# Values one step behind the next step's scores, and the second batch's keys one step later, in a four-layer kernel of window attention and experts

## The reference

```python
x = x + einsum('bct,bcd->bdt', x, weights[cond])        # layer 0: one 64x64 matrix per batch, over tokens
x = x + attention(x)                                     # layer 1: 8 heads, 4 kv groups, paged cache, window of 256
x = x + (einsum('bsi,bio->bso', x, W[id]) + b[id])       # layer 2: one of 16 experts (512x512) per batch
x = x + (x @ W3.T + scale * (x @ A[ad].T) @ B[ad].T)     # layer 3: dense 512x512 and an adapter of rank 16
```

```python
scores = einsum('bghtd,bgsd->bghts', qg, k_all) * SCALE
allowed = (kpos <= pos) & (kpos > pos - 256)
p = softmax(where(allowed, scores, -inf))
o = einsum('bghts,bgsd->bghtd', p, v_all);  out = o @ Wo.T
```

## Time and profile before

| | |
|---|---|
| median of 3 runs | 1145.85 us (1144.73 to 1155.21) |
| the profiled execution | 1151.32 us, of which the profile's span is 1149.5 us |
| PE busy over the span | 1043.8 us, 91% |
| PE weight loads | 702.4 us, 61% |
| DVE, ACT, POOL busy | 57%, 47%, 47% |
| granted clock of TensorE, mean | 0.962 |
| DMA, mean | 171 GB/s |

### The profile page before, as it was taken

How to read it: one execution, slowest core, us unless ns; L and a number is a source line. 1 busy time by engine, 2 the same in 40 slices (tenths; PEclk the granted TensorE clock), 3 DMA queues, 4 the chain that set the end, 5 groups by cost and what they waited for, 6 DMA issues and landing times.

```text
span 1149.5 us, 23649 instructions
## 1 busy us (share of the span) xinstructions
PE 1043.8 (91%) x6354; PEld 702.4 (61%) x6354; DVE 653.0 (57%) x1887; ACT 539.1 (47%) x1336; POOL 535.4 (47%) x601
## 2 busy tenths in 40 slices
PE   4999999997488999999899999998999999999997
PEld 2776777775355666656566566665655666656655
DVE  5889796667234555545455555555454554545552
ACT  3457766674333445434344444444354443434440
POOL 2555445368545545544544445544454545444400
PEclk9999999999559999989999999999899998999998
DMA  3343534553356666555656666666566666566640
GB/s 127 106 150 115 165 114 149 158 196 123 93 170 214 208 185 218 182 177 167 189 184 208 196 185 208 182 188 204 172 198 187 189 204 185 169 188 206 201 147 19
DMA packets 95335, 196.13 MB, mean 171 GB/s; under 512 B 31346, under 2 KB 40114, under 8 KB 87110
## 3 DMA queue, kind: packets, MB, share of 16 engines
q1 hardware_dynamic: 63942, 149.49, 40.0%
q0 software_dynamic: 30784, 44.16, 13.9%
q10 hardware_dynamic: 576, 2.10, 0.5%
HBM read 195.08 MB, written 33.56 MB: 199 GB/s over the span
## 4 chain that ended last, share of the span: by engine, by line
PE 62%; ACT 4%; issue 3%; another core or an unknown queue 3%; DMA 1%; POOL 1%; DVE 0%; ACTq 0%; POOLq 0%; DVEq 0%
PE bank L93 22%; PE bank L1341 10%; PE bank L1316 9%; PE bank L1303 8%; PE bank L1295 8%; PE bank L1282 4%; ACT KT L1101 2%; PE bank L1272 2%; ACT PT L1101 1%; DMA KV<-kv_scratch,idxs 1%; DMA KV<-in_pool,idxs 1%; ACT PR L1110 0%; POOL KV L1007 0%; POOL KVE L1017 0%
## 5 line engine op out<-in xcount | busy, mean ns | idle before, releaser
L1101 ACT ACTIVATE PT<-bank 112x384 f32<-112x384 f32 x256 | 113.5, 487 | 267.1 <-PE bank L1303 205.1
L1179 DVE CUSTOM_DVE_ANT_0 SM<-bank,FM 128x336 f32<-128x336 f32 x256 | 129.7, 507 | 168.1 <-PE bank L1295 131.1
L1017 POOL DMA_INDIRECT KVE<-kv_scratch,idxs_e x96 | 95.7, 997 | 124.9 <-DMA KVE<-in_pool,idxs_e 100.1
L1017 POOL DMA_INDIRECT KV<-kv_scratch,idxs x96 | 95.8, 998 | 119.4 <-DMA KV<-in_pool,idxs 99.9
L1110 ACT ACTIVATE PR<-SM,nb 128x336 f32<-128x336 f32 x256 | 145.4, 574 | 1.1 <-DVE nb L1183 0.9
L1007 POOL DMA_INDIRECT KV<-in_pool,idxs x96 | 95.0, 990 | 76.2 <-PE bank L1316 49.6
L1007 POOL DMA_INDIRECT KVE<-in_pool,idxs_e x90 | 88.9, 988 | 87.5 <-PE bank L1316 59.7
L1101 ACT ACTIVATE KT<-bank 128x336 f32<-128x336 f32 x128 | 57.5, 449 | 145.3 <-PE bank L1282 137.7
L1341 PE MATMUL bank<-W,XT 128*64 128x512 f32 x512 | 123.7, 604 | 0.7 <-ACT XT L1101 0.7
L1295 PE MATMUL bank<-KT,QB 64*128 64x336 f32 x512 | 112.9, 519 | 11.2 <-ACT KT L1101 9.0
L1303 PEld LDWEIGHTS bank<-ident,PR 128*112 128x112 f32 x768 | 85.1, 137 | 48.7 <-issue 47.8
(11 more groups left out here) (173 smaller groups left out, 2139.7 us busy)
## 6 DMA issues: line engine op xcount, KB each, us to landing
W<-in_w SPq DMA_DIRECT2D x64, 1024.0 KB
FM<-mask SPq DMA_DIRECT2D x64, 168.0 KB
X<-in_x SPq DMA_DIRECT2D x32, 256.0 KB
x_scratch<-X SPq DMA_DIRECT2D x32, 256.0 KB
kv_scratch<-KVR SPq DMA_DIRECT2D x32, 256.0 KB
qt_scratch<-QT SPq DMA_DIRECT2D x32, 256.0 KB
QB<-qt_scratch SPq DMA_DIRECT2D x32, 256.0 KB
XB<-x_scratch SPq DMA_DIRECT2D x32, 256.0 KB
```

The lines of the kernel that those rows point to most:

```text
L1017: pool.indirect_dma_start(out=KV[k][:, c, :], out_offset=None, in_=kv_d, in_offset=bass.IndirectOffsetOnAxis(ap=idxs[k][:, NCH + c:NCH + c ...
L1101: return nc.scalar.activation(dst, src, ACT.Copy)
L1179: v.tensor_tensor_reduce(out=SM[u % 2][:, :], in0=bank[u % 2][:, 0:SPAN], in1=FM[k][:, :], scale=1.0, scalar=-3e38, op0=ALU.add, op1=ALU.m ...
```

## The change

Three things are moved. First, `values` j of a pair goes from right behind `turn` 2j, 2j + 1 to behind the next step's scores: values 0 behind scores 2, values 1 behind scores 3, values 2 and 3 into the next body, behind its scores 0 and 1. Second, keys 2 go from stage 0 to stage 1, keys 3 stand ahead of the output's second half, and the keys of the next pair stand one half of the expert earlier. Third, what ACT and DVE do is put in an order that goes with it: on ACT the exps stand ahead of the copies of the turned probabilities of the step before, and `turn_x(XB2)` with its copy XT2 comes behind scores 3 and its exps. There are four PR tiles instead of two. No instruction is added or taken away.

```diff
-            PR = [sbt(f"PR{i}", [P, SPAN]) for i in range(2)]
+            PR = [sbt(f"PR{i}", [P, SPAN]) for i in range(4)]
...
                 def exp(p, u):
                     act.wait_ge(s_m, at(p, 8, u))
-                    wait(act, s_ptp, p * 8 + u - 1)
-                    nc.scalar.activation(PR[u % 2][:, :], SM[u % 2][:, :], ACT.Exp, bias=nb[:, u:u + 1],
+                    wait(act, s_ptp, p * 8 + u - 3)
+                    nc.scalar.activation(PR[u % 4][:, :], SM[u % 2][:, :], ACT.Exp, bias=nb[:, u:u + 1],
...
# ACT
+                        exp(p, 0)
+                        exp(p, 1)
                         probs(q, 6)
                         probs(q, 7)
-                        exp(p, 0)
-                        exp(p, 1)
+                        exp(p, 2)
+                        exp(p, 3)
                         heads(q, 1)
-                        keys(pr, 1, 0)
                         probs(p, 0)
                         probs(p, 1)
-                        exp(p, 2)
-                        exp(p, 3)
+                        keys(pr, 1, 0)
+                        exp(p, 4)
+                        exp(p, 5)
                         probs(p, 2)
                         probs(p, 3)
-                        exp(p, 4)
-                        exp(p, 5)
                         keys(pr, 1, 1)
+                        exp(p, 6)
+                        exp(p, 7)
                         heads(p, 0)
                         act.wait_ge(s_x2p, at(q, 1, 0))
                         copy(XT2[:, :, :, :].rearrange("p k b t -> p (k b t)"), bank[7][:, :]).then_inc(s_xt2, 1)
                         probs(p, 4)
                         probs(p, 5)
-                        exp(p, 6)
-                        exp(p, 7)
...
# DVE: heads(q, 1) behind masked 2, 3; norm 2 ahead of the add to XB2; masked 6, 7 ahead of heads(p, 0), norm 3, XBB, x3
...
# PE
                         turn_x(XB3, s_x3p)
+                        values(before, 2)
                         turn(q, 6)
                         turn(q, 7)
-                        pe.wait_ge(s_kt, at(p, 4, 1))
-                        keys(pr, 1, 0)
-                        values(before, 3)
...
                         scores(pr, 1)
+                        values(before, 3)
                         turn(p, 0)
                         turn(p, 1)
+                        pe.wait_ge(s_kt, at(p, 4, 1))
+                        keys(pr, 1, 0)
                         dense3(2, KC, False)
...
-                        values(pr, 0)
...
                         scores(pr, 2)
+                        values(pr, 0)
                         turn(p, 2)
                         turn(p, 3)
-                        output(q, 2, KC)
-                        values(pr, 1)
                         pe.wait_ge(s_kt, at(p, 4, 2))
                         keys(pr, 1, 1)
+                        output(q, 2, KC)
+                        scores(pr, 3)
+                        values(pr, 1)
                         pe.wait_ge(s_x2, at(q, 1, 0))
                         turn_x(XB2, s_x2p)
-                        scores(pr, 3)
                         turn(p, 4)
                         turn(p, 5)
-                        expert(before, 0, 2)
-                        values(pr, 2)
                         pe.wait_ge(s_kt, at(p, 4, 3))
                         keys(pr.move(1), 0, 0)
-                        expert(before, 2, KC)
+                        expert(before, 0, 2)
                         pe.wait_ge(s_kt, at(p + 1, 4, 0))
                         keys(pr.move(1), 0, 1)
+                        expert(before, 2, KC)
```

More of the change, by code:

```diff
@@ L1128, in body @@
                         copy(XTH3[:, :, :].rearrange("p k t -> p (k t)"), bank[7][:, :]).then_inc(s_xt3h, 1)
+                    if attention:
+                        exp(p, 0)
+                        exp(p, 1)
                     if dense:
@@ L1189, in norm @@
                     for g2 in range(2):
-                        v.tensor_scalar(PR[g2][:, :], PR[g2][:, :], rinv[:, 2 * j + g2:2 * j + g2 + 1], None,
+                        pr_ = PR[(2 * j + g2) % 4]
+                        v.tensor_scalar(pr_[:, :], pr_[:, :], rinv[:, 2 * j + g2:2 * j + g2 + 1], None,
                                         ALU.mult).then_inc(s_pn, 1)
@@ L1213, in body @@
                         norm(p, 0)
-                    if dense:
-                        heads(q, 1)
                     if adapted:
@@ L1229, in body @@
                         masked(pr, 3)
+                    if dense:
+                        heads(q, 1)
                     if attention:
@@ L1240, in body @@
                         masked(pr, 5)
+                        norm(p, 2)
                     if dense:
@@ L1245, in body @@
                     if attention:
-                        norm(p, 2)
+                        masked(pr, 6)
+                        masked(pr, 7)
                         heads(p, 0)
+                        norm(p, 3)
                     if dense:
@@ L1252, in body @@
                         v.tensor_tensor(XBB[:, :], XB2[:, :], BB[:, :], ALU.add).then_inc(s_xbb, 1)
-                    if attention:
-                        masked(pr, 6)
-                        masked(pr, 7)
-                        norm(p, 3)
-                    if dense:
                         dve.wait_ge(s_xbb, at(q, 1, 0))
@@ L1303, in turn @@
                         last = nc.tensor.transpose(bank[2 + u % 2][0:CH, c * P:(c + 1) * P],
-                                                   PR[u % 2][:, c * CH:(c + 1) * CH], ident[:, :])
+                                                   PR[u % 4][:, c * CH:(c + 1) * CH], ident[:, :])
                     last.then_inc(s_ptp, 1)
@@ L1394, in body @@
                         scores(pr, 2)
+                        values(pr, 0)
                         turn(p, 2)
                         turn(p, 3)
+                        pe.wait_ge(s_kt, at(p, 4, 2))
+                        keys(pr, 1, 1)
                     if dense:
@@ L1399, in body @@
                     if attention:
+                        scores(pr, 3)
                         values(pr, 1)
-                        pe.wait_ge(s_kt, at(p, 4, 2))
-                        keys(pr, 1, 1)
                     if dense:
```

## The result

The changed kernel took 1163.34 us (median of 5 runs, 1159.33 to 1176.82), the kernel before 1146.34 us beside it (5 runs, 1144.73 to 1155.21): a ratio of 1.016, 95% interval 1.012 to 1.020. Slower, as forecast, and 2.7 us from the forecast of 1166.

The account below looks back on a forecast made before the run. PE, busy 91% of the span, was taken to bound the kernel. To 1151.3 us it added 7.5 (bodies of 25.78 us), 3.5 for edge bodies and 4 for late signals and half clock: 1166 us, range 1144 to 1188.

Parts of the forecast that it names:

- Values: PE's 34.1 us idle ahead of values in bodies 2 to 30 (14.5 smooth, 19.6 in lumps) would go.
- (a): Expert in stage 3 waits for XT2, copied on ACT behind exps 6 and 7: 1.11 us a body.
- (b): Scores 3 wait for ACT's KT copy, behind exps 4 and 5 and two PT copies: 0.35 us a body.
- (c): After the next body's scores 0, PE waits for DVE's add to XB3: 0.23 us a body.
- (d): Layer 3's small matmuls wait for XTL3, written by DVE behind two masked units: 0.41 us a body.
- The residual of late signals and half clock: What stays in bodies 2 to 30 of late PE signals and PE work at half clock: 4 us.
- The edge bodies: Bodies 0, 1 and 31, outside the stretch, get the same new waits: 1.17 us each, 3.5 us.
- Costed at nothing: Keys 2 in stage 1, OTL, PR tiles, gathers, W2 loads and next queries: covered, no added time.
- The falling clock: Rival: the new stage 3 wait brings half clock, 3.14 us each in half of 29 bodies: 1207 us; chance 0.11.
- PE's weight loads as a measure of free time: Rival: weight loads fill 62% of the stretch, so PE's free 38% absorbs new waits: 1146 us; chance 0.04.
- Faster: Rival: waits removed outweigh those added, with an XT2 wait of 0.1 us and no lumps: 1133 us; chance 0.11.
- even: Rival: each of four new waits is 0.15 us shorter and no lumps stay: 1145 us; chance 0.14.

Follow-up runs that it names:

- e4: Kernel before with only the values, and the heads that depend on them, one step later: 1127.99 us, 1.009 of the kernel before.
- e2: Changed kernel with PE's keys 1 of the next pair behind the whole expert: 1148.23 us, 1.026 of the kernel before.
- e3: Changed kernel with XT2 copied ahead of exps 6 and 7 and the next pair's keys 1 behind the whole expert: 1139.67 us, 1.022 of before.
- e1: Changed kernel with ACT copying XT2 ahead of exps 6 and 7: 1139.96 us, 1.020 of the kernel before.
- e9: e1 with SP loading the next queries ahead of its wait for XB2: 1157.17 us, 1.012 of the kernel before.
- e5: e3 with SP loading the next queries ahead of the store and the wait for XB2: 1144.49 us, 0.993 of the kernel before.
- c_after2: Changed kernel run again unchanged, on the third chip: 1165.69 us, 1.019 of the kernel before.
- c_after: Changed kernel run again unchanged, on the second chip: 1168.54 us, 1.016 of the kernel before.
- e6: Changed kernel rearranged: XT2 before exps, output's second half behind values 0, keys 2 in stage 0, next keys moved, queries early: 1138.76 us, 0.989 of before.
- e8: Kernel before with each gather in the loop bringing 32 of 112 rows: 1186.57 us, 1.040 of the kernel before.
- c_before: Kernel before run again unchanged, on the second chip: 1164.82 us (single).

## Why the prediction was right, point by point

**Values.** The 34.1 us at values went to 0.0, and PE's busy time fell by 9.5 us with the half clock (11.5 forecast at most). Right. e4 shows that the first comes of the values' place alone (on the chip without late signals, so for the smooth wait and not for the lumps).

**The four new waits.** Right in place and order, too high in sum:

| wait | forecast | smooth bodies | stretch, forecast | stretch, measured |
|---|---|---|---|---|
| (a) XT2, expert | 1.11 | 0.94 to 1.02 | 32.2 | 30.4 |
| (b) KT, scores 3 | 0.35 | 0.40 to 0.42 | 10.2 | 17.0 with other scores |
| (c) XB3, turn_x | 0.23 | 0.10 to 0.16 | 6.7 | 3.4 |
| (d) XTL3, small matmuls | 0.41 | 0.07 to 0.18 | 11.9 | 3.9 |
| sum of a body | 2.10 | 1.53 to 1.76 | | |

The step that was mis-sized is PE's side of (d), and less of (c). The timetable took starts that follow each other from the body of before. In the new order six transposes of the turns stand ahead of a small matmul and not of keys, and take 0.87 us up to it, not 0.66; turn_x to values takes 0.58 and not 0.49. PE comes 3.20 us behind scores 0, not 2.96, and the chain ends at 3.27, not 3.37, so it waits less; the work is in the same 23.67 us. In (a) PE's side was right to the last digit (3.18 us); the chain was 4.12 and not 4.29 us. That (a) is XT2's place on ACT is shown on the first chip: with the copy moved, the wait goes from 28.5 to 0.0 us (e2, e3), and it is 0.0 in e1. On the other chips the late signal of turn_x would keep up a part of it (11.7 us in e9, 23.8 in e5).

**The body and the lumps.** Forecast 25.78 us a body, measured 25.20 and about 25.4 by turns: 29 x 25.3 = 734 us instead of 747.6. The residual of late signals and half clock, put at 4 us, was 745.4 - 734 = 11 us (five bodies of 26.7 to 28.3 us hold 10 of it). One term 14 us too high, one 7 us too low: the stretch came out at 745.4 and 751.5 us in two executions, against 751.6. That the total is so near is luck in part: two misses that cancel.

**The edge bodies.** Forecast +3.5 us. Measured in c_after2 against before: bodies 0 and 1 +3.2 us, the end +1.4 us, and +3.0 us in the first part, which the change doesn't touch (over the 14 profiles it takes 302.4 to 306.6 us, with the same code). With the stretch's +5.3 that makes the 13.0 us between the spans. So 3 of the forecast's 15 us came from a place that it had not in its sum.

**Costed at nothing.** Keys 2 cost nothing but in lumps (1.5 us at scores 2 in 2 bodies). OTL, PR, gathers and W2: no idle time in the groups. The queries cost 1.3 us here, as said, but only because the body had become long; 12.8 us in e3. In bodies 0 and 1, outside the stretch, c_after waits 3.7 us more for them.

**The rivals.** The falling clock didn't come: the granted clock is 1.00 over the stretch, though every body has the hole in stage 3. The half clock came at longer waits, in few bodies: in c_after2 in body 3 behind 2.50 us at the expert (and at the start of body 2, from a wait ahead of it), in c_after in body 3 behind 2.98 us at keys and in body 26, whose expert waits 3.57 us. PE's weight loads as a measure of free time: the body of 25.20 us is its 23.67 us of work and its waits, to 0.01 us, with the weight loads at 15.45 us. Faster and even lie outside the three intervals of the change (1.012 to 1.020, 1.009 to 1.023, 1.011 to 1.027), but for the first tenth of a per cent of the second.

**The range.** Its upper end of 1188 us is said to be the sum with 20 us of lumps instead of 4; that sum is 1182 us. The measured time lies inside either way.

**The comparison depends on the chip.** The kernel before has a smooth body of 24.4 us and lumps on top; the changed one 25.3 us and fewer. Without its lumps before would be at 1151.3 - (740.1 - 29 x 24.36) = 1118 us, which is what it took on the first chip, though no profile of it there shows that this is the reason. That the four kernels profiled there have hardly a late signal fits it. On such a chip the change should cost 29 x 0.9 = 26 us (an estimate; the nearest run there, e2, is 29.9 us over the kernel before), on the others it gives part of it back by smoother running.

## What to carry to other kernels

When an instruction is moved in an in-order queue, write down for each of its neighbours what it covered and what now stands ahead of it on every queue, SP's too: here 34.1 us of waits and 9.5 us of half clock did go, and the places behind them took 49 us. An idle time shown in front of one instruction is not what its removal wins; take the second latest chain off first (0.94 us was worth 0.6, over two chips, and the 28.5 us of e2 were worth 14.3 on one). When signals come late at random, work that covers a wait is worth more than the mean of the wait shows (this is argued: e6 has such cover nearly everywhere and won on a chip with late signals, but no run varies the cover alone). Two kernels should be compared on one chip, and on more than one: the expectations of e1, e3 and e4 failed in part because they set a time of one chip against a profile of another.

## What the runs showed that wasn't expected

PE's completion signals came up to 4.5 us behind the modelled end of their instruction (body 13 above). Late ones are in the ten profiles that were not taken on the first chip, whatever the kernel and with thinner transfers too, and hardly in the four that were; what in the chip causes them is open. The same kernel took 1118, 1142, 1146 and 1153 us in the median in four sets of runs. The length of a wait doesn't decide alone whether the clock falls: in e8 a wait of 1.52 us kept the full clock and one of 1.48 us was followed by the half clock, the 2.13 us of body 13 above kept it, and in c_before (body 30) one of 1.08 us was followed by the half clock, where the prediction had put the least at about 1.5 us.
